# Per-token output scales in a quantised feed-forward block: one product of 32 columns with masked copies, instead of four products of 8 columns

## The chip, the cores and the metric

The kernel is one program on one core of a Trainium2 chip. The metric is the device time of one execution in microseconds, median over repeated executions. The core's engines are TensorE (PE: matrix products, with weight loads, PEld, beside them), VectorE (DVE), ScalarE (ACT), GpSimd (POOL) and SyncE (SP), which here only issues transfers. Each runs its own list of instructions in order and waits for the others through semaphores.

## The reference, cut to what matters

```python
x = x + tanh(g_xattn) * xattn(layernorm(x), ctx)      # 16 batches, 128 tokens, 512 features
x = x + tanh(g_ffn)   * ffn(layernorm(x))

def h_bitlinear(x, w):                 # used three times: gate, up, down
    xq = act_quant(fwht(x))            # Hadamard transform, then 8 bits with one scale per token
    wq = weight_quant(w)               # ternary, one scale per matrix
    return xq @ wq.T
ffn(h) = h_bitlinear(silu(h_bitlinear(h, w_gate)) * h_bitlinear(h, w_up), w_down)
```

`act_quant` takes the largest absolute value of a token's transformed row, divides by 127, rounds, and multiplies the scale back. The change concerns this last factor for the down projection: one number for each of the 512 tokens of a unit.

## The kernel before, in words

The program has two halves. In the first, `attention(step)` runs over the 16 batches, and the feed-forward weights are made ternary beside it. The second runs over `NU = 4` units of `UB = 4` batches, 512 tokens each. For unit u:

- `gate_up(u)` on PE: 16 blocks `ob` of 128 hidden features, each a `rows` call for gate and one for up (4 products of 512 columns each, L886). DVE multiplies the gate rows by the scales (`gate`, L1486), ACT applies silu (L1180), DVE multiplies by the up rows (`hidden`, L1491). Gate rows use two PSUM banks in turn, so gate block 15 can only start when DVE has taken gate block 13 out.
- `transform(u, nxt)`: the Hadamard transform of the hidden values in two steps (L940, then L952 and L954), while `quantise_input(nxt, ...)` transforms and quantises the next unit's input (L822, L829, L839, L840). DVE splits the first step's result (`low`, L1466) and takes maxima (`peak`, L1505).
- the chain of scales of unit u, inside `gate_up(u+1)`. At `ob == 4` PE transposes the maxima (L921). At `ob == 5` `chain` on DVE brings them to one row per group of 8 tokens (`NG = 64` groups by `T8 = 8` tokens): L1512, L1515, L1517, L1519 (reciprocal), L1520 (`cz[:, 4, :]`, the factor for the output) and L1523 (`q_sc`, the factor for rounding, 64 by 128). At `ob == 7` `chain_back` on PE spreads both over the 128 partitions: one transpose (L926), and for the output factors four products of 8 columns (L928), one for each batch, with `gmt[:, tb, :]` as the stationary side: a mask of 64 by 128 that is 1 where token p of batch tb belongs to group g. `chain_end` on DVE copies the result (L1528 `z_sc`, L1529, L1532).
- `scale(u)` on POOL multiplies the transformed values by `z_sc` in 8 pieces (L579). ACT rounds pieces 0 and 1 (L1198, L1200). DVE rounds the others (L1536): pieces 2 and 3 after blocks 12 and 13, and in the loop pieces 4 and 5 after blocks 14 and 15, and 6 and 7 after the last. SP transposes each rounded piece by a transfer (L360).
- `project(u)` on PE: the down projection (L963), after which DVE adds the scaled result to x (`output`, L1542).
- then `front_statistics` on DVE (L1277), `front_scales` (L539 to L546) and `front` (L557 to L564) on POOL, with `apply` on ACT (L1174) between them, which make the input that PE turns at the start of the next transform (`first_turn`, L822).

For u = 0 and 1 PE, DVE and POOL run this in a loop. The third chain stands written out in `gate_up(last_u)`. The fourth stands in the tail: `project_kept` and `chain_back(last_u)` alternate on PE, and `scale` is divided between ACT (L1254) and DVE (L1633). All orders are fixed by hand. So `chain_back` runs four times, and the rounding beside `scale` on POOL three times.

Of the kernel before, what the change touches and what calls it, by code (L numbers as in the profile page):

```python
# [8 lines left out]
ALU = mybir.AluOpType  # L9
ACT = mybir.ActivationFunctionType  # L10
AX_X = mybir.AxisListType.X
# [15 lines left out]
UB = 4  # L27
NU = NB // UB
UT = UB * P
T8 = P // NC  # L30
NG = UT // T8
# [26 lines left out]
def reach(eng, sem, value):  # L58

    if not isinstance(value, int) or value > 0:  # L60
        eng.wait_ge(sem, value)


def reach_apart(eng, past, *pairs):

    values = [v if isinstance(v, int) else eng.to_reg(v) for _, v in pairs]
    eng.wait_ge(past, 1)
    for (sem, _), v in zip(pairs, values):
        reach(eng, sem, v)


def flamingo_block(nc, x, k_t, v, w, gates, ident, had, had16, g_mask, g_mask_t, t_mask, out):
    with ExitStack() as ctx:
        def sb(name, shape, dt):
            return ctx.enter_context(nc.sbuf_tensor(name, shape, dt))
# [3 lines left out]
        def sem(name):  # L79
            if name not in sems:  # L80
                sems[name] = ctx.enter_context(nc.semaphore(name))
            return sems[name]


        ps = ctx.enter_context(nc.psum_tensor("ps", [P, 8, 512], F32))
# [79 lines left out]
        ones_f = sb("ones_f", [P, P], F32)  # L165
        gm = sb("gm", [P, NG + 3 * (P // T8)], F32)
        gmt = sb("gmt", [NG, UB, P], F32)
        t8m = sb("t8m", [P, T8], F32)
        mv = sb("mv", [P, 2 + UB, 2], F32)
        ve = sb("ve", [P, 2 + UB], F32)  # L170
# [17 lines left out]
        cz = sb("cz", [NG, 6, T8], F32)  # L188
# [403 lines left out]
        def _(pe):  # L592
# [329 lines left out]

            def chain_back(u):

                reach_apart(pe, sem("ones_set"), (sem("c_qs"), u.times(2, 2)))
                pe.transpose(ps[:, 5, 0:NG], diag[0:NG, :], ident_f[0:NG, 0:NG])  # L926
                for tb in range(UB):
                    last = pe.matmul(ps[:, 5, NG + T8 * tb:NG + T8 * tb + T8], gmt[:, tb, :], cz[:, 4, :],  # L928
                                     start=True, stop=True)
                last.then_inc(sem("c_t2"), 1)  # L930

            def transform(u, nxt):

# [77 lines left out]
            pe.transpose(ps[0:NG, 4, 0:P], mz[:, :], ident_f[:, :]).then_inc(sem("c_t1"), 1)  # L1011
            project_kept(1, 3, 12)
            chain_back(last_u)
            project_kept(1, 12, NC)
            project_kept(2)
# [243 lines left out]
        def _(dve):  # L1259
# [61 lines left out]
            def finish(n, kvh):  # L1321

                if not exists(n):
                    return
                dve.wait_ge(sem("to_done"), 2 * n + kvh + 1)
                reach(dve, sem(f"x1_done{kvh}"), n)
                t = T_BANK.rearrange("p (h s) -> p s h", s=SLOT)
                dve.reciprocal(r_sum[:, kvh, :], t[:, D, :]).then_inc(sem("rsum_done"), 1)
                dve.wait_ge(sem("rsum_done"), 2 * n + kvh + 1)
                dve.scalar_tensor_tensor(att[kvh], t[:, 0:D, :], tg[:, 0:1], r_sum[:, kvh, :].unsqueeze(1).broadcast_to([P, D, HALF]),  # L1330
                                         ALU.mult, ALU.mult).then_inc(sem("fin_done"), 1)
# [57 lines left out]
            def absolute(h):  # L1389
                loaded(dve, h)  # L1390
                dve.tensor_reduce(part[:, h:h + 1], w_half(h), AX_X, ALU.add, apply_absolute_value=True
                                  ).then_inc(sem("abs_dve"), 1)
# [90 lines left out]
            def gate(u, ob):  # L1483
                reach(dve, sem("g_done"), u.times(NC, ob + 1))
                reach(dve, sem("h_done"), u.times(NC, ob + 1 - GS))
                dve.tensor_tensor(gs[ob % GS], ps[:, G_BANKS[ob % 2], :], s_row, ALU.mult).then_inc(sem("gs_done"), 1)  # L1486

            def hidden(u, ob):
                reach(dve, sem("silu_done"), u.times(NC, ob + 1))
                reach(dve, sem("u_done"), u.times(NC, ob + 1))  # L1490
                dve.tensor_tensor(X[:, :, ob, :], ps[:, U_BANKS[ob % 3], :].rearrange("p (g t) -> p g t", g=NG),  # L1491
                                  gs[ob % GS].rearrange("p (g t) -> p g t", g=NG), ALU.mult).then_inc(sem("h_done"), 1)
# [6 lines left out]
            def peak(u, q):  # L1499

                peak_of(u, 8 * q, 8 * q + 8)

            def peak_of(u, g0, g1):
                reach(dve, sem("z_out"), u.times(16, g1 // 4))
                dve.tensor_reduce(mz[:, g0:g1], Z[:, g0:g1, :], AX_X, ALU.max,  # L1505
                                  apply_absolute_value=True).then_inc(sem("mz_done"), 1)

            def chain(u):

                c = sem("c_step")  # L1510
                dve.wait_ge(sem("c_t1"), u.times(1, 1))
                dve.tensor_reduce(cz[:, 0, :], ps[0:NG, 4, 0:P].rearrange("g (t c) -> g t c", c=NC), AX_X, ALU.max  # L1512
                                  ).then_inc(c, 1)
                dve.wait_ge(c, u.times(4, 1))
                dve.tensor_tensor(cz[:, 1, :], cz[:, 0, :], su[:, 1, :], ALU.mult).then_inc(c, 1)  # L1515
                dve.wait_ge(c, u.times(4, 2))
                dve.tensor_scalar(cz[:, 2, :], cz[:, 1, :], 1.0 / QMAX, EPS / (QMAX * C_I), ALU.mult, ALU.max).then_inc(c, 1)  # L1517
                dve.wait_ge(c, u.times(4, 3))
                dve.reciprocal(cz[:, 3, :], cz[:, 2, :]).then_inc(c, 1)  # L1519
                dve.tensor_scalar(cz[:, 4, :], cz[:, 2, :], wsd_tg[0:NG, :], QMAX * C_I, ALU.mult, ALU.mult  # L1520
                                  ).then_inc(sem("c_qs"), 1)
                dve.wait_ge(c, u.times(4, 4))
                dve.tensor_tensor(q_sc[:, :, :], cz[:, 3, :].unsqueeze(2).broadcast_to([NG, T8, NC]),  # L1523
                                  su[:, 1, :].unsqueeze(2).broadcast_to([NG, T8, NC]), ALU.mult).then_inc(sem("c_qs"), 1)

            def chain_end(u, f_tok=f_tok):
                dve.wait_ge(sem("c_t2"), u.times(1, 1))
                dve.tensor_copy(z_sc[:, :], ps[:, 5, 0:NG]).then_inc(sem("c_sc"), 1)  # L1528
                dve.tensor_tensor(f_sel[:, :, :], ps[:, 5, NG:NG + UB * T8].rearrange("p (b t) -> p b t", b=UB),  # L1529
                                  t8m[:, :].unsqueeze(1).broadcast_to([P, UB, T8]), ALU.mult).then_inc(sem("c_rd"), 1)  # L1530
                dve.wait_ge(sem("c_rd"), u.times(1, 1))
                dve.tensor_reduce(f_tok[:, :], f_sel[:, :, :], AX_X, ALU.add).then_inc(sem("c_f"), 1)  # L1532

            def rounding(u, p, q=q_z):
                dve.wait_ge(sem("z_scaled"), u.times(8, p + 1))
                dve.tensor_scalar(q[:, 8 * p:8 * p + 8, :], Z[:, 8 * p:8 * p + 8, :], MAGIC, MAGIC,  # L1536
                                  ALU.add, ALU.subtract).then_inc(sem("rounded"), 1)
# [23 lines left out]
            def gates_and_chain(u, prev, more=False):  # L1561
                reach(dve, sem("a2_done"), u.times(16))
                for ob in range(NC):
                    gate(u, ob)
                    if ob == 1 and prev is None:
                        dve.wait_ge(sem("signed"), 12)
                    if prev is not None and ob == 7:
                        chain_end(prev)
                    if ob > 0:
                        hidden(u, ob - 1)  # L1570
                    if prev is None:
                        if ob in DOWN_DVE:
                            absolute(DOWN_DVE[ob])
                        if ob == 0:
                            finish(NB - 1, 0)
                        if ob == 1:
                            finish(NB - 1, 1)
                            dve.wait_ge(sem("gm_done"), 1)
                            dve.tensor_copy(su[:, 0, :], ps[0:NG, G_PLACE, 0:T8]).then_inc(sem("f_su"), 1)
                        if ob == 8:  # L1580
                            down_scale()
                    else:
                        if ob < 3:
                            peak(prev, 5 + ob)
                        if ob == 5:
                            chain(prev)
                        if 12 <= ob < 14:
                            rounding(prev, ob - 10)
                        if more and ob >= 14:
                            rounding(prev, ob - 10)  # L1590
                hidden(u, NC - 1)

            gates_and_chain(Index(None, 0), None)
            dve.wait_ge(sem("x1_done0"), NB)
            dve.wait_ge(sem("x1_done1"), NB)
            with dve.Fori(0, NU - 2) as i:
# [10 lines left out]
            kept_u, u = Index(None, NU - 2), Index(None, NU - 1)  # L1607
# [96 lines left out]
```

## Time and profile before

| what | value |
|---|---|
| median of 3 runs | 466.92 us (466.58 to 470.59) |
| the profiled execution | 466.68 us |
| its span in the profile | 464.8 us |
| TensorE busy | 450.1 us, 97% of the span |
| VectorE busy | 382.1 us, 82% |
| granted TensorE clock | full, in all 40 slices |

The profiled execution's own time is 1.9 us longer than its span; that part lies before the first and after the last instruction. PE's busy time contains modelled ends of overlapping products, so 97% says that PE is rarely without work, not that it is at its peak.

### The profile page before, as it was taken

The page shows a single profiled execution, that of the slowest core. Times are in us where ns is not written, and L with a number is a line of the kernel's source. Part 1 is how long each engine was busy: PE and PEld are TensorE (multiplying, and loading weights), DVE is VectorE, ACT ScalarE, POOL GpSimd, SP SyncE. Part 2 cuts the span into 40 slices and gives each one's busy share as a digit, 9 for nine tenths or more (in the row PEclk, how much of TensorE's full clock was granted, in tenths as well). Part 3 has the DMA queues.
Part 4 walks back from the last instruction along what each step waited for, and adds up shares of the span by engine and source line. Part 5 has one row for each costly group of instructions (what it writes and reads, how often), then busy time and mean ns, then how long its engine had stood idle before and what let it go on. Part 6 is the DMA issues. An engine that isn't in the chain of part 4 may idle for free.

```text
span 464.8 us, 9025 instructions
## 1 busy us (share of the span) xinstructions
PE 450.1 (97%) x3112; PEld 285.9 (61%) x3112; DVE 382.1 (82%) x703; ACT 293.5 (63%) x522; POOL 214.6 (46%) x331
## 2 busy tenths in 40 slices
PE   8999999999999989989999999999999999999997
PEld 7655555554555434469844578954469964479664
DVE  5889998787968749859998967998976999888892
ACT  3498987677768779877747327643616753657460
POOL 4355556988997544755007634203926200920000
PEclk9999999999999999999999999999999999999999
DMA  8999120022023050001100650100460110242077
GB/s 249 328 349 350 35 52 18 17 59 25 13 42 103 17 188 5 1 1 25 24 0 6 117 149 11 23 12 0 83 158 31 24 25 0 41 90 53 1 146 216
DMA packets 68183, 35.90 MB, mean 77 GB/s; under 512 B 50288, under 2 KB 62960, under 8 KB 68144
## 3 DMA queue, kind: packets, MB, share of 16 engines
q1 hardware_dynamic: 67408, 34.48, 28.9%
q10 hardware_dynamic: 736, 0.92, 0.6%
q8 instruction: 22, 0.36, 0.3%
q14 instruction: 17, 0.14, 0.1%
HBM read 19.26 MB, written 4.19 MB: 50 GB/s over the span
## 4 chain that ended last, share of the span: by engine, by line
PE 74%; POOL 8%; issue 6%; DVE 6%; ACT 4%; DMA 1%; POOLq 0%; DVEq 0%; ACTq 0%
PE ps L886 16%; PE ps L963 12%; PE ps L940 11%; PE ps L615 7%; PE ps L637 5%; PE ps L680 5%; PE ps L952 3%; PE ps L954 3%; PE ps L697 3%; PE ps L829 2%; PE ps L645 2%; PE ps L822 1%; PE ps L739 1%; DVE wst L1491 1%; DVE wst L1486 1%
## 5 line engine op out<-in xcount | busy, mean ns | idle before, releaser
L886 PE MATMUL ps<-wst 128*128 128x512 bf16 x512 | 113.1, 379 | 2.3 <-DVE wst L1486 2.0
L1317 DVE TENSOR_REDUCE reg<-ps 128x4 f32<-128x512 f32 x128 | 81.7, 683 | 22.9 <-PE ps L637 21.3
L886 PEld LDWEIGHTS ps<-wst 128*128 128x128 bf16 x512 | 49.2, 98 | 62.3 <-DVE wst L1486 4.0
L579 POOL TENSOR_TENSOR reg_rest<-reg_rest,z_sc 128x1024 f32<-128x1024 f32 x24 | 47.4, 2010 | 82.7 <-DVE z_sc L1528 82.7
L1044 ACT ACTIVATE reg<-ps 128x512 f32<-128x512 f32 x116 | 62.9, 597 | 25.1 <-PE ps L645 24.8
L637 PE MATMUL ps<-reg 32*128 32x256 f32 x512 | 72.6, 400 | 0.3 <-ACT reg L1071 0.2
L1180 ACT ACTIVATE wst<-wst 128x512 f32<-128x512 f32 x64 | 40.1, 628 | 51.6 <-DVE wst L1486 51.2
L615 PE MATMUL ps<-reg 32*128 32x512 f32 x232 | 70.1, 639 | 0.0
L940 PE MATMUL ps<-had_f,wst 128*128 128x128 f32 x512 | 67.1, 276 | 1.1 <-DVE wst L1491 1.1
L940 PEld LDWEIGHTS ps<-had_f,wst 128*128 128x128 f32 x512 | 64.0, 191 | 4.4 <-DVE wst L1491 1.8
L1210 ACT CAST y_split<-ps 128x512 fp32r<-128x512 f32 x64 | 37.4, 586 | 34.0 <-PE ps L940 34.0
L1466 DVE TENSOR_TENSOR y_split<-ps,y_split 128x512 fp32r<-128x512 f32 x64 | 43.5, 684 | 15.7 <-ACT y_split L1210 15.7
L1486 DVE TENSOR_TENSOR wst<-ps,wst 128x512 f32<-128x512 f32 x64 | 43.7, 682 | 8.3 <-PE ps L886 8.3
L637 PEld LDWEIGHTS ps<-reg 32*128 32x128 f32 x512 | 46.0, 184 | 2.2 <-ACT reg L1071 0.7
L1491 DVE TENSOR_TENSOR wst<-ps,wst 128x512 f32<-128x512 f32 x64 | 43.5, 680 | 1.4 <-ACT wst L1180 1.3
L963 PE MATMUL ps<-wst,reg_rest 128*128 128x512 bf16 x192 | 42.8, 380 | 0.0
L1219 ACT COPY reg_rest<-ps 128x512 f32<-128x512 f32 x64 | 37.9, 592 | 2.1 <-PE ps L954 1.7
L1505 DVE TENSOR_REDUCE mz<-reg_rest 128x8 f32<-128x1024 f32 (+1 forms) x33 | 38.3, 1174 | 0.2 <-issue 0.2
L471 POOL TENSOR_TENSOR x_all<-x_all,reg 128x256 f32<-128x256 f32 x32 | 24.2, 756 | 28.2 <-DVE reg L1330 28.1
L963 PEld LDWEIGHTS ps<-wst,reg_rest 128*128 128x128 bf16 x192 | 27.4, 145 | 13.9 <-issue 0.5
L615 PEld LDWEIGHTS ps<-reg 32*128 32x128 f32 x232 | 21.5, 183 | 21.1 <-ACT reg L1044 10.2
L680 PE MATMUL ps<-reg 128*32 128x512 f32 x256 | 34.1, 604 | 0.1
(171 smaller groups left out, 747.6 us busy)
## 6 DMA issues: line engine op xcount, KB each, us to landing
wst<-in_w SPq DMA_DIRECT2D x16, 512.0 KB, 8.4
reg<-in_w SPq DMA_DIRECT2D x8, 512.0 KB, 5.1
out<-x_all SPq DMA_DIRECT2D x16, 256.0 KB, 2.1
x_all<-in_x SPq DMA_DIRECT2D x3, 1024.0 KB, 8.8
reg<-in_v SPq DMA_DIRECT2D x4, 256.0 KB, 4.4
reg<-in_k_t SPq DMA_DIRECT2D x28, 32.0 KB, 2.6
x_all<-in_x ACTq DMA_DIRECT2D x1, 512.0 KB, 4.3
reg_rest<-reg SPq DMA_TRANSPOSE x20, 3.0
```

The costliest lines, as they stand in the source:

```text
L579: pool.tensor_tensor(z, z, sc, ALU.mult).then_inc(sem("z_scaled"), 1)
L615: pe.matmul(ps[:, column_bank(c, m), :], kpad[b // CHUNK % 2][strip(i), b % CHUNK, a, :], q_t[b % 4][strip(i), :], start=True, stop=False)
L637: last = pe.matmul(ps[:, row_bank(r, m), 256 * g:256 * g + 256], q_t[n % 4][strip(i), P * h:P * h + P], kpad[n // CHUNK % 2][strip(i), n % ...
L680: last = pe.matmul(O_BANK[SLOT * l:SLOT * l + SLOT, :], v_pad[n // CHUNK % 2][:, n % CHUNK, 4 * kvh + l, :], probs[:, 4 * kvh + l, :], sta ...
L886: last = pe.matmul(ps[:, banks[ob % n], :], tern_gu[:, ob // 2, m, j, P * (ob % 2):P * (ob % 2) + P], q1_t[:, j, :], start=(j == 0), stop= ...
L940: last = pe.matmul(ps[:, Y_BANKS[s % 3], P * k:P * k + P], X[:, 4 * s + k, :, :].rearrange("p c t -> p (c t)"), had_f[:, :], start=True, s ...
L963: last = pe.matmul(ps[:, bank, :], q2.rearrange("p g (t c) -> p c (g t)", c=NC)[:, c, P * tb:P * tb + P], tern_d[:, c, :], start=(c == 0), ...
L1044: act.activation(probs[:, 2 * j + m, :], ps[:, column_bank(c, m), :], ACT.Exp, scale=D ** -0.5).then_inc(sem("exp_done"), 1)
L1317: dve.tensor_reduce(neg_max[n % 2][:, g:g + 2, i + m, :], ps[:, row_bank(r, m), :].rearrange("p (g a t) -> p g a t", g=2, a=2), AX_X, ALU. ...
L1466: dve.tensor_tensor(y_low[s % RING], ps[:, Y_BANKS[s % 3], :], y_high[s % RING].bitcast(F32), ALU.subtract).then_inc(sem("y_low"), 1)
L1486: dve.tensor_tensor(gs[ob % GS], ps[:, G_BANKS[ob % 2], :], s_row, ALU.mult).then_inc(sem("gs_done"), 1)
L1491: dve.tensor_tensor(X[:, :, ob, :], ps[:, U_BANKS[ob % 3], :].rearrange("p (g t) -> p g t", g=NG), gs[ob % GS].rearrange("p (g t) -> p g t ...
```

## The change

`chain_back` now has one product of 32 columns. Its stationary side is `g_any`, the sum of the four masks. Its moving side `cz_by` (64 by 32) holds four copies of the 8 factors, each multiplied by `g_block[g, b]`, which is 1 where group g belongs to batch b. `group_masks` makes `g_any` and `g_block` once on DVE, between unit 0's `gate_up` and the loop, out of the loaded masks and in their place. `chain` has one more DVE instruction, which makes `cz_by`, ahead of the one that makes `q_sc`. PE now waits for three counts of `c_qs` per chain where it waited for two.

```diff
+        g_any = gmt[:, 0, :]
+        cz_by = gmt[:, 1, 0:UB * T8].rearrange("g (b t) -> g b t", b=UB)
+        g_block = gmt[:, 2, 0:UB]
...
             def chain_back(u):
-                reach_apart(pe, sem("ones_set"), (sem("c_qs"), u.times(2, 2)))
+                reach_apart(pe, sem("ones_set"), (sem("c_qs"), u.times(3, 3)))
                 pe.transpose(ps[:, 5, 0:NG], diag[0:NG, :], ident_f[0:NG, 0:NG])
-                for tb in range(UB):
-                    last = pe.matmul(ps[:, 5, NG + T8 * tb:NG + T8 * tb + T8], gmt[:, tb, :], cz[:, 4, :],
-                                     start=True, stop=True)
-                last.then_inc(sem("c_t2"), 1)
+                pe.matmul(ps[:, 5, NG:NG + UB * T8], g_any, cz_by.rearrange("g b t -> g (b t)"), start=True, stop=True
+                          ).then_inc(sem("c_t2"), 1)
...
+            def group_masks():
+                dve.wait_ge(sem("const_in"), 16 * 5)
+                dve.tensor_reduce(cz[:, 4, 0:UB], gmt[:, :, :], AX_X, ALU.max).then_inc(sem("g_masks"), 1)
+                dve.wait_ge(sem("g_masks"), 1)
+                for b in range(1, UB):
+                    dve.tensor_tensor(g_any, g_any, gmt[:, b, :], ALU.add).then_inc(sem("g_masks"), 1)
+                    dve.wait_ge(sem("g_masks"), b + 1)
+                dve.tensor_copy(g_block, cz[:, 4, 0:UB]).then_inc(sem("g_masks"), 1)
+                dve.wait_ge(sem("g_masks"), UB + 1)
...
                 dve.wait_ge(c, u.times(4, 4))
+                dve.wait_ge(sem("c_qs"), u.times(3, 1))
+                dve.tensor_tensor(cz_by, cz[:, 4, :].unsqueeze(1).broadcast_to([NG, UB, T8]),
+                                  g_block.unsqueeze(2).broadcast_to([NG, UB, T8]), ALU.mult).then_inc(sem("c_qs"), 1)
                 dve.tensor_tensor(q_sc[:, :, :], ...
...
             gates_and_chain(Index(None, 0), None)
+            group_masks()
```

In PE's order inside the loop this is the end of gate block 7, the chain's way back and up block 7, before:

```order
L882 REGISTER_ALU
L886 MATMUL ps<-wst 128x512 x4
L66 ISA
L926 MATMUL ps<-ident_f,diag 128x64
L928 MATMUL ps<-cz,gmt 128x8 x4
L886 MATMUL ps<-wst 128x512 x4
```

and now:

```order
L885 REGISTER_ALU
L889 MATMUL ps<-wst 128x512 x4
L66 ISA
L929 MATMUL ps<-ident_f,diag 128x64
L930 MATMUL ps<-gmt 128x32
L889 MATMUL ps<-wst 128x512 x4
```

Nothing changes its place; four products have become one.

In DVE's order inside the loop, the chain's last steps and the gate block behind them, before:

```order
L1517 TENSOR_SCALAR cz<-cz 64x8
L1519 RECIPROCAL cz<-cz 64x8
L1520 TENSOR_SCALAR cz<-cz,few 64x8
L1523 TENSOR_TENSOR diag<-cz,su 64x128
L61 REGISTER_ALU
L1486 TENSOR_TENSOR wst<-ps,wst 128x512
```

and now:

```order
L1529 TENSOR_SCALAR cz<-cz 64x8
L1531 RECIPROCAL cz<-cz 64x8
L1532 TENSOR_SCALAR cz<-cz,few 64x8
L1535 ISA
L1536 TENSOR_TENSOR gmt<-cz,gmt 64x32
L1538 TENSOR_TENSOR diag<-cz,su 64x128
L61 REGISTER_ALU
L1487 TENSOR_TENSOR wst<-ps,wst 128x512
```

A wait and a product of 64 by 32 stand between the output factor and `q_sc`, and so ahead of every gate and hidden block that follows.

## Rows read from the trace of the kernel before

**Rows 1.** The page: busy time, share of the span, instructions.

```profile
PE 450.1 (97%) x3112; PEld 285.9 (61%) x3112; DVE 382.1 (82%) x703; ACT 293.5 (63%) x522; POOL 214.6 (46%) x331
```

**Rows 2.** The chain that ended last, 240 to 250 us: start, length, what.

```profile
245.95 0.20 PE ps L926
246.15 0.85 PE ps L928 x8
247.00 3.13 PE ps L886 x14
```

**Rows 3.** Timeline of the weight loads there: start, length, engine, instruction.

```profile
245.88 1.02 PEld L928 LDWEIGHTS ps<-cz,gmt 64*128 64x128 f32 x8
```

**Rows 4.** The chain that ended last, 300 to 325 us.

```profile
304.54 0.21 PE ps L840 x2
```

**Rows 5.** Timeline of DVE, 245 to 250 us, with idle time and releaser.

```profile
245.05 0.17 DVE L1520 TENSOR_SCALAR cz<-cz,few 64x8 f32<-64x8 f32 x1
245.16 0.28 DVE L1523 TENSOR_TENSOR diag<-cz,su 64x128 f32<-64x128 f32 x1
...
247.16 0.21 DVE L1528 COPY z_sc<-ps 128x64 f32<-128x64 f32 x1
247.29 0.17 DVE L1529 TENSOR_TENSOR f_sel<-ps,t8m 128x32 f32<-128x32 f32 x1
```

**Rows 6.** Timeline of DVE, 255 to 268 us.

```profile
255.77 0.69 DVE L1486 TENSOR_TENSOR wst<-ps,wst 128x512 f32<-128x512 f32 x1 [0.36 <-PE ps L886]
...
256.98 2.19 DVE L1536 TENSOR_SCALAR reg<-reg_rest 128x1024 bf16<-128x1024 f32 x1
...
260.29 1.18 DVE L1536 TENSOR_SCALAR reg<-reg_rest 128x1024 bf16<-128x1024 f32 x1
261.40 0.68 DVE L1486 TENSOR_TENSOR wst<-ps,wst 128x512 f32<-128x512 f32 x1
...
264.90 0.68 DVE L1536 TENSOR_SCALAR reg<-reg_rest 128x1024 bf16<-128x1024 f32 x1
...
267.30 0.68 DVE L1277 BATCH_NORM_STATS2 few<-x_all 128x6 f32 x1
```

**Rows 7.** Line L1536: min/median/max ns, first and last start.

```profile
L1536 DVE TENSOR_SCALAR reg<-reg_rest x14: 677/1182/2267, 257.0 to 407.2; 128x1024 bf16<-128x1024 f32 x14
```

**Rows 8.** Timeline of POOL, 255 to 263 us.

```profile
256.73 1.90 POOL L579 TENSOR_TENSOR reg_rest<-reg_rest,z_sc 128x1024 f32<-128x1024 f32 x1
258.58 2.35 POOL L579 TENSOR_TENSOR reg_rest<-reg_rest,z_sc 128x1024 f32<-128x1024 f32 x1
260.89 2.34 POOL L579 TENSOR_TENSOR reg_rest<-reg_rest,z_sc 128x1024 f32<-128x1024 f32 x1
```

**Rows 9.** Timeline of PE near block 15, in three units.

```profile
259.83 2.76 PE L886 MATMUL ps<-wst 128*128 128x512 bf16 x12 [0.64 <-DVE wst L1486]
...
333.28 2.76 PE L886 MATMUL ps<-wst 128*128 128x512 bf16 x12 [0.67 <-DVE wst L1486]
...
406.74 2.76 PE L886 MATMUL ps<-wst 128*128 128x512 bf16 x12 [0.71 <-DVE wst L1486]
```

**Rows 10.** Timeline of POOL and PEld, 271 to 278 us.

```profile
271.25 0.24 POOL L539 TENSOR_SCALAR ve<-mv 128x4 f32<-128x4 f32 x1 [8.02 <-DVE mv L1279]
...
276.43 0.73 POOL L564 TENSOR_TENSOR scratch4k<-wst 128x256 f32<-128x256 f32 x1
277.28 0.42 PEld L822 LDWEIGHTS ps<-ident_f,scratch4k 128*128 128x128 f32 x4 [0.18 <-issue]
```

**Rows 11.** Timeline of the tail's chain, and the chain that ended last behind it.

```profile
439.89 0.23 DVE L1528 COPY z_sc<-ps 128x64 f32<-128x64 f32 x1 [1.01 <-PE ps L928]
...
439.85 21.75 PE ps L963 x100
```

**Rows 12.** Timeline of all engines, 204 to 207 us.

```profile
204.69 0.69 DVE L1466 TENSOR_TENSOR y_split<-ps,y_split 128x512 fp32r<-128x512 f32 x1 [1.80 <-ACT y_split L1210]
...
206.01 0.48 PE L952 MATMUL ps<-y_split,had_r 128*128 128x512 f32 x1
```

## The prediction

> **What bounds the kernel now.** I read the page first. PE is busy 97% of the span [rows 1], so time can mostly be won only where PE has less to do or waits less. The chain that ended last shows it around the changed step: down-projection, gate and up products without a gap, and in their middle 0.20 us for the transpose and 0.85 us for the four small products, which leave 8 records (two for each float32 product) [rows 2]. The bf16 products of block 7 follow at once. So `chain_back` lies on the path that sets the end. The timeline of PE then shows where PE waits in the same stage: once in each of the three `gate_up` calls that carry a chain, for 0.64, 0.67 and 0.71 us, in front of its last 12 products (gate block 15, up 14, up 15), and what releases it is DVE's gate block 13 [rows 9]. To see why that is late I read DVE and POOL together. DVE starts its first rounding, which I call R2 (piece 2), at 256.98 us, and it takes 2.19 us, where the same instruction takes 0.68 when POOL is idle [rows 6, 7]. POOL's piece there runs from 256.73 us and the next begins at 258.58; R2 ends at 259.17, 0.59 after that. The next rounding ends at 261.47, 0.58 after POOL's next start at 260.89, and the POOL pieces that began when a rounding ran are 2.35 and 2.34 us long instead of 1.90 [rows 6, 8]. **So a rounding gets in only between two POOL pieces, and R2 missed such a place by 0.25 us** and waited for a whole piece. The longest of the 14 roundings is 2.27 us, in the third unit [rows 7]; each unit has one such R2.
>
> The Trainium skill says the same in SBUF — State Buffer, section "SBUF: two separate sides": the port pair that VectorE and GpSimd share is an exclusive lock, held for the whole instruction. The rows above agree; what follows goes by the rows.
>
> **PE's saving.** Records fall from 8 to 2. By the chain that ended last one costs 0.85 / 8 = 0.106 us [rows 2], and a product of 8 columns elsewhere costs 0.21 us for its two records [rows 4]. The weight side stays 64 by 128, so I take 0.21 us for the one product of 32 columns as well: the saving is 6 x 0.106 = **0.64 us** in each of four chains. Upper bound: by the weight loads, 1.02 / 8 = 0.13 each [rows 3], 0.76 us. Lower bound: if 0.85 us were a fixed cost of the change to 64 rows and back, nothing; the two-record product at 0.21 us speaks against that.
>
> The Trainium skill, TensorE: Matmul & The Clock Gate, section "Part 2: What happens when you issue a matmul", gives some 81 ns from product to product in a stream with weight loads at 128 columns. By that page six records would be 0.49 us, and the four chains 1.9 instead of 2.6 us; the row is of this very product, so it decides.
>
> **DVE's extra instruction.** `cz_by` must wait for the factor's instruction (0.17 us, and some 0.03 for the wait), and `q_sc` follows 0.13 us behind it, the distance at which independent small instructions start here. That puts `q_sc` 0.33 us behind L1520, where it stood 0.11 behind [rows 5]: **0.22 us later**. The width, 64 by 32, is like the 128 by 32 product that takes 0.17 us [rows 5]. At worst it costs like the 64 by 128 one, 0.28 us, with a further 0.1 for the register step of the wait: 0.4. Does PE wait for it? `q_sc` ended at 245.44, and PE's weight load for the transpose began at 245.88, when its bf16 products were through [rows 3, 5]: 0.44 us of cover, 0.22 left. At 0.4 it would just be used up. Behind `q_sc` on DVE stand gate 6, hidden 5, gate 7 and then `z_sc`. `z_sc` began at 247.16 with no idle time ahead of it [rows 5], so DVE's own queue sets it, not the products: **POOL's scaling starts 0.22 us later, although PE is 0.64 us earlier.** By gate 12 DVE waits for PE again (0.36 us idle) [rows 6], so from there on DVE follows PE.
>
> **R2 against POOL's pieces.** R2 becomes ready at 256.98 - 0.64 = 256.34. POOL's place at 256.73 moves to 256.95. R2 is then 0.61 us early where it was 0.25 late; it gets in at 256.95 and ends at 257.54 instead of 259.17. Gate 13 is taken out by about 258.15, and PE wants it at 259.19 - 0.64 = 258.55: **PE's wait goes**. PE is thus 0.64 + 0.64 = 1.28 us earlier at the end of block 15. The other two units have the same pattern (0.67 and 0.71 us).
>
> **What is late next.** POOL's pieces that meet a rounding are 2.31 us apart, so the next places are at 259.26, 261.57 and 263.88. The roundings behind are ready at 258.66, 260.97 and 263.28, and each waits 0.60 us. The block after a rounding starts 0.51 us after its place, as at 261.40 after 260.89 [rows 6, 8]. So hidden 15 starts at 264.39; before, the rounding at 264.90 took a slot of 0.60 and hidden 15 came at 265.50. The statistics (L1277) start 1.1 us earlier than at 267.30 [rows 6]. POOL's front waits 8.02 us for these statistics, and PE's first turn in the next transform starts at 277.28, 0.12 us after POOL's last front piece ends, PE having been ready for 0.18 us [rows 10]. So in the two loop units the gain is capped by this path: **1.1 us each, not 1.28**. The transposes by SP have the cover they had within some 0.3 us, over 1 us each, and PE never waited for them. The third unit has no such front behind it: its gain is 0.64 + 0.71 = **1.35 us**. In the tail `z_sc` waited 1.01 us for the products, and 21.75 us of products without a gap follow to the end [rows 11]: the full **0.64 us**, since DVE's 0.22 leave 0.79 us of that idle time.
>
> **The masks, once.** A reduce of 64 by 512 (0.68 us, as full-width DVE instructions here), three dependent additions of 64 by 128 (0.28 + 0.03 each, by L1523), one copy (0.15): some 1.8 us. DVE was idle there for 1.80 us up to 204.69, waiting for ACT, and the result that it then makes by 205.38 is taken by PE only at 206.01 [rows 12]: 2.4 us of cover. Cost 0; if the masks took 1 us more than I count, 0.2 to 0.4 us.
>
> **Sum.** 1.1 + 1.1 + 1.35 + 0.64 = 4.2 us off the profiled execution's 466.68: 462.5. That execution lies 0.24 us under the median of 466.92, so the median goes to **462.7 us**, 0.9% less. With PE's saving at 0.76 it is 0.2 lower (the loop units stay capped); with the skill's page, 0.3 higher; with DVE's addition at 0.4 instead of 0.22, 0.4 to 0.6 higher, because POOL's later start holds the front back.
>
> **Rivals.** (a) PE's saving counts, but its wait stays. If R2 is not let in at the earlier place, because POOL, which always has a piece ready, goes first, R2 still waits for the place at 258.58 + 0.22 = 258.80. Gate 13 then comes at the old time plus 0.22: the wait swallows the saving in three units, and only the tail's 0.64 us is left: 3 x 0.22 - 0.64 = 0, 466.9 us. Against it: at 258.58 and 260.89 R2 and its successor did get in between two pieces with POOL's next ready. (b) The two engines don't lock but slow each other while they overlap: R2 then takes its 2.2 us wherever it falls, PE's wait stays as it is, and the gain is 4 x 0.64 = 2.6: 464.3 us, or up to 465.0 if POOL's later start is paid for in each unit. For it: POOL's pieces do become longer. Against it: both roundings end 0.58 to 0.59 after a POOL start. (c) More than I sum: the front is not the cap, and a record costs 0.13: 4 x 0.76 + 0.64 + 0.67 + 0.71 = 5.1, 461.9 us. It needs statistics that start 1.4 us earlier, against three more waits of 0.6 us. (d) The other side: the products' time is not that of the records. If one product of 64 rows takes as long as four, PE gains nothing, POOL starts 0.22 us later, and R2 moves only 0.22 us against POOL's pieces where it lacks 0.25. It misses again, and every unit ends 0.22 us later, with up to 1 us more if the masks are not covered: 467.6 to 468.6 us. The point from which it decides is a saving on PE under about 0.05 us in `chain_back`. (e) That the change doesn't do what it says: one product is issued per chain, and only if it leaves 8 records is this (d).
>
> **How the numbers follow.** The forecast with its bounds has a chance of 0.62, (a) 0.08, (b) 0.15, (c) 0.08, (d) with (e) 0.07. The range for 8 in 10 is 461.5 to 465.0: it holds the forecast, (b) and (c) and leaves (a) and (d) out. A measurement of this kernel tells about 1% from no change, and 1% is 4.7 us, to 462.25. Faster by over 1%: all of (c) and a fifth of the forecast's own spread, 0.20. Slower by over 1%, above 471.6, is dearer than (d) at its dearest: 0.02, for what I have not seen. Within 1%: 0.78.
>
> **What the profile of the changed kernel would show.** One group for the new product, 8 records in the whole trace where L928 had 32, at 0.11 us each in the chain. `z_sc` starts 0.2 us later against L1520 in three chains, and in the tail its idle time of 1.01 us falls to about 0.15. R2 takes 1.2 us, not 2.2, in all three units, and PE's wait before its last 12 products is gone. In the loop units five POOL pieces take 1.90 us and three 2.3 us, where it was six and two. PE's first turn waits some 0.2 us more for POOL's front in the loop units. If R2 is still 2.2 us long, (a), (b) or (d) holds, and the time of gate 13 says which. I would be wrong above all if PE's start of block 12 does not move, or if the extra DVE instruction costs PE its 0.44 us of cover.

## The result, and the profile after

The changed kernel takes 462.10 us (median of 4 runs, 461.99 to 462.30), against 466.75 us before (median of 4 runs): the ratio of the runs is 0.9896, 95% interval 0.9868 to 0.9924. The profiled execution took 462.05 us, with a span of 460.2 us; the span is 4.6 us shorter. The granted TensorE clock is full in all 40 slices. A few executions of several versions, the kernel before among them, showed a mean granted clock of 0.985 to 0.993 and took 2 to 8 us longer; the medians below include them, the spreads leave them out.

The page, busy time by engine, answers to [rows 1]:

```profile
PE 448.3 (97%) x3088; PEld 284.6 (62%) x3088; DVE 383.6 (83%) x712; ACT 293.3 (64%) x522; POOL 214.9 (47%) x331
```

24 product records are gone from PE, which is the 6 in each of four chains, and DVE has 9 more: the extra product four times and the five mask steps. PE's busy time, in which the ends of products are modelled, fell by only 1.8 us. By the chain that ended last (below) the products themselves give 4 x 0.65 = 2.6 us of the 4.6, and the rest is waiting that is gone.

The chain that ended last, 240 to 250 us, answers to [rows 2]: start, length, what.

```profile
245.86 0.20 PE ps L929
246.06 0.20 PE ps L930 x2
246.26 3.77 PE ps L889 x17
```

The new product takes 0.20 us for its two records; the four took 0.85.

The timeline of DVE around the chain answers to [rows 5]: start, length, engine, instruction.

```profile
244.98 0.17 DVE L1532 TENSOR_SCALAR cz<-cz,few 64x8 f32<-64x8 f32 x1
245.19 0.18 DVE L1536 TENSOR_TENSOR gmt<-cz,gmt 64x32 f32<-64x32 f32 x1
245.30 0.28 DVE L1538 TENSOR_TENSOR diag<-cz,su 64x128 f32<-64x128 f32 x1
...
247.30 0.21 DVE L1543 COPY z_sc<-ps 128x64 f32<-128x64 f32 x1
```

`q_sc` starts 0.32 us behind the factor, where it was 0.11; `z_sc` comes at 247.30, 0.14 us later on the clock although the chain began 0.07 us earlier. It is still set by DVE's queue.

The timelines of POOL (first the row of all eight pieces, then two single ones) and DVE at the roundings answer to [rows 6, 8]:

```profile
247.58 16.23 POOL L582 TENSOR_TENSOR reg_rest<-reg_rest,z_sc 128x1024 f32<-128x1024 f32 x8 [27.67 <-DVE z_sc L1543]
...
256.86 2.34 POOL L582 TENSOR_TENSOR reg_rest<-reg_rest,z_sc 128x1024 f32<-128x1024 f32 x1
259.16 2.34 POOL L582 TENSOR_TENSOR reg_rest<-reg_rest,z_sc 128x1024 f32<-128x1024 f32 x1
```

```profile
256.24 1.20 DVE L1551 TENSOR_SCALAR reg<-reg_rest 128x1024 bf16<-128x1024 f32 x1
...
258.56 1.18 DVE L1551 TENSOR_SCALAR reg<-reg_rest 128x1024 bf16<-128x1024 f32 x1
...
266.09 0.68 DVE L1278 BATCH_NORM_STATS2 few<-x_all 128x6 f32 x1
```

R2, the first rounding, starts 0.62 us ahead of POOL's piece at 256.86, gets in there, and ends at 257.44: 1.20 us long, not 2.19. A "place" is, here as in the prediction, the moment at which POOL's next piece starts. POOL's undisturbed pieces start (256.86 - 247.58) / 5 = 1.856 us apart, so the sixth piece, which is R2's place, comes 5 x 1.856 = 9.28 us after the first. The line's longest rounding is now 1.277 us, not 2.267. PE, which waited three times for DVE in front of its last 12 products [rows 9], doesn't any more; that stretch is one row without idle time:

```profile
254.84 6.21 PE L889 MATMUL ps<-wst 128*128 128x512 bf16 x28
```

What is late next is the front, as in [rows 10]. PE's weight load for the first turn of the next transform:

```profile
276.06 0.42 PEld L825 LDWEIGHTS ps<-ident_f,scratch4k 128*128 128x128 f32 x4 [0.50 <-issue]
```

It starts 1.22 us earlier than before and now stands idle 0.50 us ahead, not 0.18: POOL's last front piece, at 275.20 us and 0.73 long, ends at 275.93.

Where the time went, by the same points in the two chains that ended last (starts in us; the last column is what the stage between two points gained; at the kept projection, `project_kept`, the third unit ends and the tail begins):

```
point                                   before    after    earlier   gained
transpose of chain 1                    245.95   245.86      0.09      0.09
first gate block of unit 2              306.15   304.90      1.25      1.16
first gate block of unit 3              379.29   376.88      2.41      1.16
transpose of chain 3                    392.78   390.10      2.68      0.27
first product of the kept projection    409.50   405.28      4.22      1.54
transpose of the tail's chain           438.80   434.82      3.98     -0.24
products behind it                      439.85   435.26      4.59      0.61
last output                             461.63   457.03      4.60      0.01
```

The first 0.09 us can't be told from scatter: the profiled executions of experiments 1 to 4 and 6 to 8 have this transpose anywhere from 245.85 to 246.14 us.

### The profile page after: what moved, and what is told of

Read it like the earlier page. It is cut to its first block, busy times and chain, and to the rows that moved or that the text cites. A ratio compares the mean times of both kernels' runs of the same rounds, so it can differ in the third digit from the quotient of the medians.

```text
span 460.2 us, 8990 instructions
## 1 busy us (share of the span) xinstructions
PE 448.3 (97%) x3088; PEld 284.6 (62%) x3088; DVE 383.6 (83%) x712; ACT 293.3 (64%) x522; POOL 214.9 (47%) x331
## 4 chain that ended last, share of the span: by engine, by line
PE 69%; POOL 9%; DVE 9%; issue 7%; ACT 4%; DVEq 0%; POOLq 0%; ACTq 0%
PE ps L889 17%; PE ps L941 11%; PE ps L618 7%; PE ps L964 5%; PE ps L640 5%; PE ps L683 5%; PE ps L953 3%; PE ps L955 3%; PE ps L700 3%; DVE wst L1492 2%; PE ps L832 2%; PE ps L648 2%; PE ps L598 2%; DVE few L1278 2%; PE ps L825 1%
```

## The experiments

Each was timed in several rounds beside the kernel before on the same chip. The kernel before had medians of 466.61 us in the first four and 466.64 us in the last four.

### 1. VectorE's half alone, on the kernel before

```diff
+                dve.wait_ge(sem("c_qs"), u.times(3, 1))
+                dve.tensor_tensor(cz_own, cz[:, 4, :].unsqueeze(1).broadcast_to([NG, UB, T8]),
+                                  gmt[:, 2, 0:UB].unsqueeze(2).broadcast_to([NG, UB, T8]), ALU.mult).then_inc(sem("c_qs"), 1)
                 dve.tensor_tensor(q_sc[:, :, :], ...
...
-                reach_apart(pe, sem("ones_set"), (sem("c_qs"), u.times(2, 2)))
+                reach_apart(pe, sem("ones_set"), (sem("c_qs"), u.times(3, 3)))
```

> The kernel before with VectorE's half of the change alone: each chain has the extra 64 by 32 product ahead of q_sc (written to an unused tile, with mask values that mean nothing, and its result read by nobody), and TensorE waits for three counts, but it still issues four products of 8 columns. The one-time mask steps are left out. The output is that of the reference. My theory (the gain is TensorE's shorter product plus a rounding that now finds an earlier place between two GpSimd pieces, because TensorE is earlier AND GpSimd later): here only GpSimd moves, by some 0.2 us, and the first rounding lacks 0.25, 0.22 and about 0.2 us in the three units, so it still misses in the first and is on the edge in the others. All missed: 3 x 0.2 = 0.6 us slower, 467.4. Caught in the third alone: some 0.9 us back, 466.5. Range 466.3 to 467.6. Rival 1 (the order of engines plays no part, the gain is TensorE's records alone): 466.75, no change. Rival 2 (the delay alone makes the gain): 464.5 or less.

Measured: 465.9 us, ratio 0.9998 (0.9975 to 1.0021). Its roundings R2 in the three units, and PE's waits, by the timelines of DVE and PE:

```profile
256.94 2.40 DVE L1540 TENSOR_SCALAR reg<-reg_rest 128x1024 bf16<-128x1024 f32 x1
...
330.66 2.32 DVE L1540 TENSOR_SCALAR reg<-reg_rest 128x1024 bf16<-128x1024 f32 x1
...
403.90 0.68 DVE L1540 TENSOR_SCALAR reg<-reg_rest 128x1024 bf16<-128x1024 f32 x1
```

```profile
260.00 2.76 PE L887 MATMUL ps<-wst 128*128 128x512 bf16 x12 [0.84 <-DVE wst L1487]
...
333.63 2.76 PE L887 MATMUL ps<-wst 128*128 128x512 bf16 x12 [0.76 <-DVE wst L1487]
```

In two units R2 misses its place and pays the 0.2 us more; in the third, which lacked least (0.18 us, against 0.25 and 0.22), it catches it and PE's wait is gone. That is the edge the theory put there. The ratio alone tells nothing from no change; the rows do, and they speak against rival 1. They speak against rival 2 as well: this delay of 0.2 us by itself doesn't do it in two units of three. The time itself missed: 465.9 us lies below the 466.5 forecast for this case and outside its range. Some 0.27 us of that comes from an idle time of DVE in the third unit, told below under "Not foreseen, a gain", which is absent here too; and the third unit gives back 0.86 us (45.16 us from its transpose to the tail's, against 46.02), where the forecast counted 0.7 net of the delay.

### 2. TensorE's half alone, on the changed kernel

```diff
-                dve.wait_ge(sem("c_qs"), u.times(3, 1))
-                dve.tensor_tensor(cz_by, cz[:, 4, :].unsqueeze(1).broadcast_to([NG, UB, T8]),
-                                  g_block.unsqueeze(2).broadcast_to([NG, UB, T8]), ALU.mult).then_inc(sem("c_qs"), 1)
...
-                reach_apart(pe, sem("ones_set"), (sem("c_qs"), u.times(3, 3)))
+                reach_apart(pe, sem("ones_set"), (sem("c_qs"), u.times(2, 2)))
```

> The changed kernel without the extra VectorE product: one product of 32 columns, whose moving side is never filled with the factors, so the output factors are left out and the output is not the reference's. TensorE waits for two counts again. Theory: TensorE is 0.65 us earlier against GpSimd's pieces, more than the 0.25 us that the first rounding lacked, so it gets in at the earlier place without the delay of GpSimd as well. Its long form (2.2 us) is gone in all three units; GpSimd starts 0.2 us earlier than in the changed kernel, which moves the statistics 0.2 us forward in the two loop units, and the tail does not wait for the extra product (0.24 us): 461.4, range 461.2 to 461.8. Rival (the delay by the extra product is needed for the better place): the 2.2 us roundings are back and TensorE waits 1.3 us in each unit, 464 or more.

Measured: 461.61 us, ratio 0.9892 (0.9878 to 0.9906). The first R2 and the tail's `z_sc`, by the timeline of DVE:

```profile
256.40 1.01 DVE L1548 TENSOR_SCALAR reg<-reg_rest 128x1024 bf16<-128x1024 f32 x1
...
434.83 0.22 DVE L1540 COPY z_sc<-ps 128x64 f32<-128x64 f32 x1 [0.36 <-PE ps L930]
```

R2 is 1.0 us long in all three units (1.01, 1.00, 1.01). So PE's shorter product is enough for the better place, the rival falls, and by the medians, taken on two occasions, the extra VectorE product costs the changed kernel about 0.5 us altogether. That fits the rows: 0.17 and 0.22 us between the transposes of the first three chains, 0.19 from the third to the tail's.

### 3. More work for GpSimd, on the kernel before

```diff
                 reach(pool, sem("c_sc"), u.times(1, 1))
+                for spare in (ident_b[:, 0:64].bitcast(F32), ident_b[:, 64:128].bitcast(F32), r_sum.rearrange("p a h -> p (a h)"))[0:3]:
+                    pool.tensor_tensor(spare, ones_f[:, 0:32], ones_f[:, 0:32], ALU.add).then_inc(sem("filled"), 1)
```

> The kernel before with three small GpSimd additions (128 by 32, results unused) ahead of each unit's eight scaling pieces; nothing else. They delay the scaling by some 0.4 to 0.6 us. Theory: more work makes the kernel faster. The first rounding, 0.25 us late before, is now early by some 0.25, and takes 0.8 to 1.0 us instead of 2.2; TensorE's wait of 0.64 to 0.71 us in front of its last 12 products goes in all three units, and the statistics start 0.8 us earlier: 0.8 + 0.8 + 0.87 = 2.5 us, 464.3, range 463.9 to 465.2. Rival (the two engines share and don't lock, so overlap costs the same wherever it falls): no gain, 466.7 to 468. Rival (the products' saving is the whole gain of the change): no gain here, 466.7.

Measured: 464.19 us, ratio 0.9949 (0.9936 to 0.9962). Timelines of POOL and DVE:

```profile
247.36 0.43 POOL L577 TENSOR_TENSOR ident_b<-ones_f 128x32 f32<-128x32 f32 x2 [27.44 <-DVE z_sc L1530]
247.75 0.24 POOL L577 TENSOR_TENSOR r_sum<-ones_f 128x32 f32<-128x32 f32 x1
247.95 1.90 POOL L581 TENSOR_TENSOR reg_rest<-reg_rest,z_sc 128x1024 f32<-128x1024 f32 x1
```

```profile
256.88 0.93 DVE L1538 TENSOR_SCALAR reg<-reg_rest 128x1024 bf16<-128x1024 f32 x1
```

The scaling starts 0.59 us after it could, and R2 takes 0.93 us (0.94 and 0.99 in the other units), with no wait of PE behind it. No product of PE and no instruction of DVE differs from the kernel before, and 2.4 us are gone. The time is within 0.2 us of the forecast. This is the clearest of the runs: half of the changed kernel's gain was to be had without the change, by a delay. Both rivals fall.

### 4. The chain's last steps earlier, on the changed kernel

```diff
                 for ob in range(NC):
+                    if prev is not None and ob == 7:
+                        chain_end(prev)
                     gate(u, ob)
                     if ob == 1 and prev is None:
                         dve.wait_ge(sem("signed"), 12)
-                    if prev is not None and ob == 7:
-                        chain_end(prev)
```

> The changed kernel with the chain's last steps on VectorE (z_sc and the two behind it) ahead of gate block 7 instead of behind it. GpSimd's scaling starts 0.6 us earlier. Plain view (earlier is better, GpSimd's end lies on the path to the next unit's input): up to 0.6 us faster in each of the two loop units, 460.9 to 461.5. Theory of places: the first rounding is ready at 256.24, and the place it used, 256.78, moves to 256.18; it is missed by some 0.06 us, the rounding waits for the next one at 258.0 and takes 2.4 us, and TensorE's wait comes back at about 0.8 us: 463.5 to 464.8. The margin is thin; if the place is still caught, the plain view's time follows from the same theory, and the length of that rounding (0.7 or 2.4 us) tells which.

Measured: 462.31 us, ratio 0.992 (0.9894 to 0.9947), with eight of its ten single executions from 461.02 to 463.51 us (464.32 and 467.82 are left out of the spread). POOL's pieces in the two loop units, R2 in the three units, and PE's one wait:

```profile
247.08 16.30 POOL L582 TENSOR_TENSOR reg_rest<-reg_rest,z_sc 128x1024 f32<-128x1024 f32 x8 [27.07 <-DVE z_sc L1543]
...
318.90 15.78 POOL L582 TENSOR_TENSOR reg_rest<-reg_rest,z_sc 128x1024 f32<-128x1024 f32 x8 [27.04 <-DVE z_sc L1543]
```

```profile
256.33 0.68 DVE L1551 TENSOR_SCALAR reg<-reg_rest 128x1024 bf16<-128x1024 f32 x1
...
328.24 2.37 DVE L1551 TENSOR_SCALAR reg<-reg_rest 128x1024 bf16<-128x1024 f32 x1
...
400.89 0.68 DVE L1551 TENSOR_SCALAR reg<-reg_rest 128x1024 bf16<-128x1024 f32 x1
```

```profile
331.27 2.76 PE L889 MATMUL ps<-wst 128*128 128x512 bf16 x12 [0.82 <-DVE wst L1487]
```

POOL started 0.50 us earlier, at 247.08, not 0.6, and the place it moved from was 256.86, not the 256.78 of the expectation. That put it at 247.08 + 9.28 = 256.36, 0.03 us after R2 was ready at 256.33: caught. In the second unit it came at 318.90 + 9.28 = 328.18, 0.06 us before R2 was ready at 328.24: missed. The third caught it. So the forecast that all three would miss was wrong in two units, where the place came some 0.2 us later than it had been put, and the run shows how sharp the edge is: a few hundredths of a microsecond decide between 0.68 and 2.37 us. The time lies between the two views' ranges, as one miss in three would have it. The single executions stand in three groups, 461.02 to 461.55 (three), 462.20 to 462.49 (four) and 463.51 (one), and the one miss seen from inside cost 1.0 us (72.65 us from the second chain's transpose to the third's, against 71.67 in experiment 7, where none is missed). None, one and two misses would look so; that reading of the groups is not shown, since only the profiled execution, 462.41 us, is seen from inside.

### 5. `q_sc` ahead of the extra product, on the changed kernel

```diff
+                dve.tensor_tensor(q_sc[:, :, :], ...).then_inc(sem("c_qs"), 1)
                 dve.wait_ge(sem("c_qs"), u.times(3, 1))
                 dve.tensor_tensor(cz_by, ...).then_inc(sem("c_qs"), 1)
-                dve.tensor_tensor(q_sc[:, :, :], ...).then_inc(sem("c_qs"), 1)
```

> The changed kernel with q_sc ahead of the extra product. TensorE's transpose needs only q_sc and its product follows it; TensorE still waits for all three counts. In the loop units and the third unit the order on VectorE costs the same, so nothing changes there. In the tail the changed kernel lost 0.24 us because TensorE waited for q_sc, and VectorE stood idle for 0.46 us ahead of the extra product. If that idle time is the dependence on the factor just computed, q_sc hides it and the time falls by 0.2 us: 461.9. If it belongs to the place in the instruction stream (a late instruction), it stays and the time is that of the changed kernel, 462.1. Both lie within this measurement's noise, the row in the trace decides.

Measured: 462.04 us, ratio 0.9885 (0.9858 to 0.9912). Its profiled execution took 468.17 us; it is 6.6 us behind the changed kernel already at the first chain's transpose (252.47 against 245.86 us), so only distances within the tail are read from it. The timeline of DVE there:

```profile
440.01 0.17 DVE L1532 TENSOR_SCALAR cz<-cz,few 64x8 f32<-64x8 f32 x1
440.12 0.28 DVE L1535 TENSOR_TENSOR diag<-cz,su 64x128 f32<-64x128 f32 x1
440.33 0.17 DVE L1538 TENSOR_TENSOR gmt<-cz,gmt 64x32 f32<-64x32 f32 x1
```

The idle 0.46 us ahead of the extra product is gone, and PE's transpose no longer waits. By the expectation that speaks for the dependence on the factor; but experiments 1 and 6 have the same dependence at the same spot, with the product 0.28 us behind the factor's start and no such idle time, so this run doesn't settle it. The time doesn't tell the two kernels apart.

### 6. Without the masks, on the changed kernel

```diff
             gates_and_chain(Index(None, 0), None)
-            group_masks()
```

> The changed kernel without the one-time mask steps (five VectorE instructions), so the one product uses the first batch's mask and values that are no block mask: the output factors are wrong for three batches of four. My view: their 1.8 us on VectorE lie in its idle time while it waits for ScalarE, and the first split is 0.3 us later at most, still ahead of TensorE's need: 462.1, within 0.15. Rival (they cost what they last, or part of it): 460.5 to 461.6. Also to be read: whether the 0.46 us of idle time ahead of the extra product in the tail stands where it stood, now that the stream of instructions is five shorter.

Measured: 461.94 us (461.80 without the four executions that spreads leave out), ratio 0.9908 (0.9879 to 0.9936). In the changed kernel the masks are these rows of DVE's timeline, and PE's first use of what follows them is the row of PE's:

```profile
202.66 0.67 DVE L1512 TENSOR_REDUCE cz<-gmt 64x4 f32<-64x512 f32 x1
203.36 0.92 DVE L1515 TENSOR_TENSOR gmt<-gmt 64x128 f32<-64x128 f32 x3
204.32 0.16 DVE L1517 COPY gmt<-cz 64x4 f32<-64x4 f32 x1
204.69 0.16 DVE L1497 COPY su<-su 64x8 f32<-64x8 f32 x1 [0.21 <-DVE gmt L1517]
204.99 0.69 DVE L1467 TENSOR_TENSOR y_split<-ps,y_split 128x512 fp32r<-128x512 f32 x1
...
205.94 0.48 PE L953 MATMUL ps<-y_split,had_r 128*128 128x512 f32 x1
```

The split ends at 205.68, PE begins at 205.94: they cost nothing that shows, and without them the first chain's transpose is no earlier (246.13 against 245.86 us). Without them the 0.46 us in the tail is gone too, with the same instructions and waits around it, which can account for the 0.2 to 0.3 us by which this kernel's median is lower:

```profile
433.89 0.17 DVE L1532 TENSOR_SCALAR cz<-cz,few 64x8 f32<-64x8 f32 x1
434.17 0.19 DVE L1536 TENSOR_TENSOR gmt<-cz,gmt 64x32 f32<-64x32 f32 x1
```

### 7. Earlier, and then late enough: three edits on the changed kernel

The edits of 4 and 5, and one of the small GpSimd additions of 3.

> The changed kernel with three edits together: the chain's last steps ahead of gate block 7, q_sc ahead of the extra product, and one small GpSimd addition (0.2 us) ahead of the scaling. With the last steps moved alone, GpSimd's place at 256.36 us stood 0.03 us behind the rounding's start at 256.33, was caught in two units and missed in one, and single executions ran from 461.0 to 464.3 us. The 0.2 us should make it safe in all three, with the pieces still 0.3 us earlier than in the changed kernel. Theory: no 2.2 us rounding in any unit, executions as close together as those of the changed kernel, and 0.3 us saved in each loop unit, as long as TensorE can use it: 461.3, range 460.9 to 461.8. Rival (the spread had another cause): the spread stays.

Measured: 461.14 us (460.74 to 462.15), ratio 0.9875 (0.9847 to 0.9903). POOL's fifth and sixth pieces in the loop units, and R2 in the three units:

```profile
254.60 4.20 POOL L584 TENSOR_TENSOR reg_rest<-reg_rest,z_sc 128x1024 f32<-128x1024 f32 x2
...
326.42 4.20 POOL L584 TENSOR_TENSOR reg_rest<-reg_rest,z_sc 128x1024 f32<-128x1024 f32 x2
```

```profile
256.33 0.71 DVE L1553 TENSOR_SCALAR reg<-reg_rest 128x1024 bf16<-128x1024 f32 x1
...
328.18 0.68 DVE L1553 TENSOR_SCALAR reg<-reg_rest 128x1024 bf16<-128x1024 f32 x1
...
399.85 0.71 DVE L1553 TENSOR_SCALAR reg<-reg_rest 128x1024 bf16<-128x1024 f32 x1
```

All three are caught with almost no wait, and the six executions lie within 1.4 us, where the eight of experiment 4 lay within 2.5 (the 464.3 of the expectation is outside that spread). The time is in the range that was forecast. It is the fastest version here, 1.0 us under the changed kernel by medians taken on different occasions; the two intervals against the kernel before overlap. R2 starts only 0.13 and 0.10 us ahead of its place in the loop units (the sixth pieces begin at 254.60 + 1.856 and 326.42 + 1.856), and its executions lie further apart than those of the changed kernel (0.3 us), against the forecast; whether the one at 462.15 missed a place isn't shown.

### 8. GpSimd later still, on the changed kernel

Six of the small additions, instead of three, in front of the scaling.

> The changed kernel with six small GpSimd additions (some 1.2 us) ahead of the scaling in each unit. Theory of places: the place before the one that it used moves to 256.2, just ahead of the rounding's start at 256.24, and the next is 1.86 us later: the rounding is 2.3 to 2.5 us long again, or 0.7 if the place slips behind its start. If long: TensorE waits 0.8 us more in each of three units and the statistics come 1.2 us later in the two loop units, 465.0 to 465.9. If the place is caught: the 1.2 us of GpSimd's delay still move its last piece and so the statistics, but TensorE doesn't wait: 463.5 to 464.5. Rival (no lock, the first half-microsecond of delay in the kernel before helped for another reason): 462.1 to 462.7, as GpSimd has 6 us of idle time behind the scaling.

Measured: 465.37 us (465.17 to 465.75), ratio 0.9967 (0.9952 to 0.9981). Timelines of POOL, DVE and PE in the first unit:

```profile
249.05 1.90 POOL L586 TENSOR_TENSOR reg_rest<-reg_rest,z_sc 128x1024 f32<-128x1024 f32 x1
...
258.32 2.34 POOL L586 TENSOR_TENSOR reg_rest<-reg_rest,z_sc 128x1024 f32<-128x1024 f32 x1
```

```profile
256.52 2.38 DVE L1555 TENSOR_SCALAR reg<-reg_rest 128x1024 bf16<-128x1024 f32 x1
```

```profile
259.56 2.76 PE L893 MATMUL ps<-wst 128*128 128x512 bf16 x12 [0.83 <-DVE wst L1491]
```

R2 missed the piece that begins at 256.47 (249.05 + 4 x 1.856) by 0.05 us and waited for the one at 258.32. R2 takes 2.37 and 2.43 us in the other units, PE's wait is back in all three (0.83, 0.82 and 0.88 us), and the time is in the range forecast for this case. On the kernel before, 0.6 us more of POOL's work won 2.4 us; on the changed kernel 1.2 us more lost 3.3 (against its median from another occasion). Of the explanations put up here, only the place between pieces gives both signs.

## Why the prediction was right, point by point

- **PE's saving**: 0.64 us per chain by the records. Measured 0.85 - 0.20 = 0.65. The row of this very product was the right one. The estimate from the 81 ns of the Trainium skill (TensorE: Matmul & The Clock Gate, section "Part 2: What happens when you issue a matmul") was 0.49 us; the trace doesn't bear it out for these float32 products.
- **DVE's extra instruction**: 0.22 us, measured 0.21 (0.32 - 0.11). `z_sc` later although PE is earlier: so it was.
- **R2's place**: forecast at 256.95, start at 256.34, end at 257.54. Measured 256.86, 256.24 and 257.44, with everything 0.09 us earlier from the first half on. PE's wait went in all three units. Experiments 3, 4 and 8 show the mechanism itself; rivals (a), (b) and (d) fall. So does (c), though its 461.9 us is nearer to the measured time than the forecast's 462.7: it needed a record at 0.13 us and a front that doesn't cap the loop units, and the rows show 0.10 and, in the next point, the cap. (e) falls by the 8 records in the whole trace, two in each chain. One part of my reason was not needed: experiment 2 shows that PE's 0.65 us alone is enough, and that POOL's delay, which widened the margin, costs time.
- **The front as the next limit**: 1.1 us each in the loop units. Measured 1.16 and 1.16, with the statistics 1.21 us earlier (266.09 against 267.30). That PE could have been earlier shows in the weight load's idle 0.50 us.
- **The third unit**: 1.35 us, measured 1.54 from its transpose to the kept projection. The mechanism was right, the size low: PE's wait of 0.71 us was followed by 12 products in 2.76 us, which take 2.61 at the pace of the products in the unbroken stretch (14.78 us for 68). I had priced the wait and not the slower start behind it, 0.15 us.
- **Not foreseen, a gain**: 0.27 us between the first gate block of unit 3 and its transpose. The kernel before has a row of DVE there, `peak`, with 0.24 us of idle time that ends with nothing shown; the changed kernel has none. The gates behind it were late for PE by it: the chain that ended last runs through DVE's gates from 382.92 to 388.25 us in the kernel before, and through PE's products alone in the changed one. The timeline of DVE in the kernel before:

```profile
378.93 2.34 DVE L1505 TENSOR_REDUCE mz<-reg_rest 128x8 f32<-128x1024 f32 x2 [0.24 <-issue]
```

- **The tail**: 0.64 us, measured 0.37. I gave the extra product no cost there because `z_sc` had 1.01 us of idle time. That was the wrong cover to look at: an earlier step, PE's transpose, waits for `q_sc`, and its cover in the kernel before was 0.51 us (`q_sc` ended at 438.22, the weight load for the transpose began at 438.73). The extra product with its 0.22 us would have left enough of it, but an idle time that I had no row for used it up, and PE waited. `z_sc`, which was to keep 0.15 us of idle time, has none.

The timelines of DVE and PE in the tail of the changed kernel:

```profile
433.65 0.17 DVE L1532 TENSOR_SCALAR cz<-cz,few 64x8 f32<-64x8 f32 x1
434.28 0.18 DVE L1536 TENSOR_TENSOR gmt<-cz,gmt 64x32 f32<-64x32 f32 x1 [0.46 <-DVE cz L1532]
434.39 0.28 DVE L1538 TENSOR_TENSOR diag<-cz,su 64x128 f32<-64x128 f32 x1
```

```profile
434.82 0.24 PE L929 MATMUL ps<-ident_f,diag 64*128 64x64 f32 x1 [0.19 <-DVE diag L1538]
```

- **The masks**: free, as forecast.
- **The sum**: 4.2 us forecast, 4.6 measured, 462.7 against 462.1. The terms that were off are the third unit (1.35, measured 1.54 and 0.27 more) and the tail (0.64, measured 0.37); the rest is the 0.09 us of the first half and 0.12 in the loop units. That the sum is so near is in part luck: the unforeseen 0.27 us won ahead of the third chain and the 0.27 us missing in the tail cancel, and both come from short idle times of DVE that the prediction didn't have. The decrease of 1.0%, 0.15 us past the bound of 462.25, is the outcome that I gave a chance of 0.2.

## What to carry to other kernels

Where one form of VectorE instruction shows very different lengths beside a long row of GpSimd instructions (here 0.68 to 2.27 us for the rounding), don't read the mean: take the longest, compare its start with the starts of the GpSimd instructions, and you see what a shift of a few tenths of a microsecond would win or lose. A shortened step on one engine is worth its length plus or minus a whole piece of the other engine, so it is worth trying a deliberate delay (experiment 3), and a version that sits within 0.05 us of such an edge, as in experiment 4, should be moved off it. Price a removed stall with the slower products behind it, and follow an added small instruction to the next wait it feeds, also where it runs outside the loop.

## What the runs showed of the hardware that I had not expected

- A 128 by 1024 rounding on VectorE beside GpSimd takes from 0.68 to 2.43 us, by its start against GpSimd's pieces: in all the rows of R2, of every kernel here, it ends 0.57 to 0.65 us after the start of a piece. It gets in at the start of GpSimd's next instruction even when that one is ready, and the GpSimd instruction takes 2.34 us instead of 1.90 for it. Ready 0.04 to 0.06 us late (experiments 1, 8 and 4), it waits 1.8 us for the next start and takes 2.37 to 2.40 us in all.
- VectorE shows short idle times that come and go with the instructions around and far ahead of them, by the one profiled execution of each kernel: 0.24 us at 378.93 us in the kernel before, and also in experiment 3, which leaves VectorE's instructions alone, but in none of the kernels whose VectorE stream differs; and 0.46 us in the tail of the changed kernel and of experiments 4 and 8, but not in 6, where five instructions far ahead are missing, nor in 5 and 7, where two are exchanged. The profile puts the 0.46 us down to the factor's instruction (L1532), but 0.40 of it has no releaser in the chain that ended last, and experiments 1 and 6 have that dependence without it. What makes these idle times stays open; no run was made on that alone.
